# An attention and mixture-of-experts kernel: order of sums, row additions and one query projection in the attention part

## The reference

```python
xn = _layernorm(x, axis=-1)
# attention
q = einsum('bte,de->btd', xn, Wq) + bq;  k = ... + bk;  v = ... + bv
dot = einsum('bqd,bkd->bqk', q, k) / sqrt(256)
z = einsum('bqk,bkd->bqd', softmax(dot, axis=-1), v)
# experts
gates = softmax(xn @ Wg.T);  scores, inds = top_k(gates, 2);  scores = scores / sum(scores)
y = sum over the 2 chosen experts of score * (silu(g) * u) @ We_down
y = y + sigmoid(xn @ Wsg.T) * shared(xn)
out = x + z + y
```

## Time and profile before

| | us |
|---|---|
| median of 3 runs (lowest, highest) | 522.28 (521.79, 523.2) |
| the profiled execution | 520.53 |
| its span, first to last instruction | 518.4 |
| PE busy | 504.4 (97%) |
| DVE busy | 395.0 (76%) |
| ACT busy | 276.1 (53%) |
| POOL busy | 239.5 (46%) |

### The profile page before, as it was taken

The page is one execution under the profiler, slowest core; times in us unless marked ns, Lnnn a source line. Parts: engine busy times, 40 slices in busy tenths (PEclk is TensorE's granted clock), DMA queues, the critical chain, the costliest instruction groups (busy, mean ns, idle before and its releaser), DMA issues.

```text
span 518.4 us, 9986 instructions
## 1 busy us (share of the span) xinstructions
PE 504.4 (97%) x3347; PEld 458.1 (88%) x3347; DVE 395.0 (76%) x831; ACT 276.1 (53%) x473; POOL 239.5 (46%) x274
## 2 busy tenths in 40 slices
PE   8999999999999979999999999998999999999997
PEld 7898999988888969899998998897898989899887
DVE  5959454779999745766665744899897979797997
ACT  4767595524665424454444445565473727272742
POOL 0171585731100676756666503357735354554650
PEclk9999999999999988999999999999999999999999
DMA  8967668841112345549655746976225823722222
GB/s 298 408 222 265 235 212 310 326 134 57 36 56 62 113 133 164 173 147 312 194 166 167 139 121 205 357 195 228 81 87 174 298 57 87 219 87 61 73 62 71
DMA packets 48464, 88.05 MB, mean 170 GB/s; under 512 B 6080, under 2 KB 27200, under 8 KB 47392
## 3 DMA queue, kind: packets, MB, share of 16 engines
q1 hardware_dynamic: 40992, 68.58, 38.4%
q0 software_dynamic: 6864, 18.75, 14.0%
q10 hardware_dynamic: 560, 0.09, 0.1%
HBM read 51.72 MB, written 35.67 MB: 169 GB/s over the span
## 4 chain that ended last, share of the span: by engine, by line
PE 79%; DVE 14%; issue 5%; ACT 1%; POOL 0%; DVEq 0%; ACTq 0%
PE ps L867 45%; PE ps L1079 12%; PE ps L873 6%; PE ps L1009 6%; PE ps L1111 6%; DVE probs_f L1704 2%; DVE pT L1375 1%; PE ps L917 1%; PE ps L1026 1%; DVE top_keys L1679 1%; DVE acc L1719 1%; ACT scored_t L1174 1%; DVE sil L1446 1%; DVE place_hot L1560 1%; DVE less_wide L1696 1%
## 5 line engine op out<-in xcount | busy, mean ns | idle before, releaser
L854 POOL DMA_INDIRECT rows_y<-ytab,slot x64 | 80.9, 1264 | 71.8 <-DVE acc L1719 51.8
L824 POOL DMA_INDIRECT blk_x<-rows,row x79 | 82.2, 1040 | 64.0 <-DVE row L1575 22.7
L867 PEld LDWEIGHTS ps<-vv,pT 128*128 128x128 f32 x768 | 94.3, 189 | 5.0 <-DVE pT L1375 2.0
L867 PE MATMUL ps<-vv,pT 128*128 128x258 f32 x768 | 95.3, 283 | 3.4 <-DVE acc L1729 1.8
L867 PE MATMUL ps<-xT,shared_w 128*128 128x512 f32 x384 | 92.7, 394 | 0.8 <-DVE sil L1446 0.6
L867 PEld LDWEIGHTS ps<-xT,shared_w 128*128 128x128 f32 x384 | 70.5, 188 | 15.8 <-issue 1.6
L867 PE MATMUL ps<-qT,xbT_hi 128*128 128x512 f32 x256 | 79.1, 390 | 0.0
L1079 PE MATMUL ps<-expert_w,blk_xT 128*128 x474 | 67.9, 293 | 1.1 <-issue 0.4
L1079 PEld LDWEIGHTS ps<-expert_w,blk_xT 128*128 128x128 f32 x474 | 60.4, 193 | 5.1 <-issue 4.8
L1363 ACT ACTIVATE probs_f<-probs_f 128x1024 f32<-128x1024 f32 x32 | 33.8, 1058 | 47.0 <-DVE probs_f L1704 39.3
L867 PEld LDWEIGHTS ps<-qT,xbT_hi 128*128 128x128 f32 x256 | 47.1, 188 | 9.4 <-issue 0.2
(11 more groups left out here) (157 smaller groups left out, 827.1 us busy)
## 6 DMA issues: line engine op xcount, KB each, us to landing
ytab<-blk_y SPq DMA_DIRECT2D x40, 256.0 KB
keys<-xT SPq DMA_DIRECT2D x8, 1024.0 KB, 4.8
vals<-vals_out SPq DMA_DIRECT2D x32, 256.0 KB, 2.9
vv<-vals SPq DMA_DIRECT2D x8, 1024.0 KB, 10.8
stage_e<-in_experts SPq DMA_DIRECT2D x16, 384.0 KB
rows<-xn SPq DMA_DIRECT2D x8, 512.0 KB, 5.0
xbT_hi<-keys SPq DMA_DIRECT2D x8, 512.0 KB
xbT_lo<-keys SPq DMA_DIRECT2D x8, 512.0 KB
```

What stands on the lines that cost most here:

```text
L824: e.indirect_dma_start(out=blk_x[:, q, n, :], out_offset=None, in_=rows, in_offset=bass.IndirectOffsetOnAxis(ap=row[:, 2 * b + n:2 * b + n ...
L854: e.indirect_dma_start(out=rows_y[:, r, k, :], out_offset=None, in_=ytab, in_offset=bass.IndirectOffsetOnAxis(ap=slot[:, k, i:i + 1], axis=0),
L867: ins = e.matmul(dst, stationary(p, k), moving(q, k), start=(n == 0), stop=(n == total - 1))
```

## The change

It reorders steps and splits two kinds in two. `weigh_sum` (reciprocal and sum in one step) becomes `sum_invert` and `weigh_sum`; `rows_in` becomes `rows_first` and `rows_second`, so that another instruction can stand between the two of a pair. Then, in the groups:
1. In group 1 the row additions of tiles 2 and 3 no longer stand ahead of tile 1's sum.
2. In groups 1 to 6 the spread comes ahead of the sum of tile `old`+1, whose reciprocal follows the spread and whose sum follows the first `less`.
3. The projection of group 7's queries moves from group 5 to group 6.
4. Row additions, reciprocals, sums and low parts of different tiles alternate.

```diff
     def weigh(n):
-        return [("weigh", n), ("weigh_sum", n)]
+        return [("weigh", n), ("sum_invert", n), ("weigh_sum", n)]
+
+    def rows_around(i, *between):
+        return [("rows_first", i), *between, ("rows_second", i), *([("gather", i + YR)] if i + YR < TILES else [])]
 
     def rows(i):
-        return [("rows_in", i), *([("gather", i + YR)] if i + YR < TILES else [])]
+        return rows_around(i)
...
-    ahead = {g: split("heads", *divmod(g + 2, 2)) for g in range(1, GROUPS - 2)}
+    ahead = {g: split("heads", *divmod(g + 2, 2)) for g in range(1, GROUPS - 3)}
+    ahead[GROUPS - 2] = split("heads", *divmod(GROUPS - 1, 2))
...
-            steps += [("tops", g), *ahead.get(g, []),
-                      *([*rows(old + 2), *rows(old + 3)] if g == 1 else []), *weigh(old + 1), *spread(g), ("less", new), ("probs", new), ("less", new + 1),
-                      *spread_second(g), ("probs_hi", new), ("probs", new + 1), *rows(new),
-                      *weigh(old + 2), ("probs_hi", new + 1), ("less", new + 2), ("probs_lo", new), *rows(new + 1),
+            if g == 1:
+                tiles = (old + 2, old + 3, new + 1, new + 3)
+            else:
+                tiles = range(new, new + CT)
+            steps += [("tops", g), *ahead.get(g, []), ("weigh", old + 1), *spread(g), ("sum_invert", old + 1), ("less", new),
+                      ("weigh_sum", old + 1), ("probs", new), ("less", new + 1),
+                      *spread_second(g), ("probs_hi", new), ("probs", new + 1), ("weigh", old + 2),
+                      *rows_around(tiles[0], ("sum_invert", old + 2)), ("weigh_sum", old + 2),
+                      ("probs_hi", new + 1), ("less", new + 2), *rows_around(tiles[1], ("probs_lo", new)),
                       ("probs", new + 2), ("less", new + 3), ("probs_lo", new + 1)]
             if g + 2 < GROUPS:
-                steps += [("probs_hi", new + 2), *weigh(old + 3), ("probs", new + 3), ("probs_lo", new + 2), *rows(new + 2),
-                          ("probs_hi", new + 3), ("probs_lo", new + 3), *rows(new + 3)]
+                steps += [("probs_hi", new + 2), ("weigh", old + 3), ("probs", new + 3),
+                          *(rows(new) if g == 1 else []),
+                          *rows_around(tiles[2], ("sum_invert", old + 3)), ("weigh_sum", old + 3),
+                          ("probs_lo", new + 2), *(rows(new + 2) if g == 1 else []), ("probs_hi", new + 3),
+                          *rows_around(tiles[3], ("probs_lo", new + 3))]
             else:
-                steps += [*rows(new + 2), *rows(new + 3)]
+                steps += [*rows(tiles[2]), *rows(tiles[3])]
...
-                elif kind == "rows_in":
+                elif kind == "rows_first":
                     i, r = a[0], a[0] % YR
                     e.wait_ge(gathered[r], 16 * TOPK * (i // YR + 1))
                     e.wait_ge(biased, i + 1)
...
+                elif kind == "sum_invert":
                     n, w = a[0], a[0] % 2
                     e.wait_ge(weighed, n + 1)
                     if n >= 2:
                         e.wait_ge(z_added, n - 1)
                     e.reciprocal(rsum[:, w:w + 1], ps[:, sum_bank(n), D:D + 1]).then_inc(sum_inverted, 1)
+                elif kind == "weigh_sum":
+                    n, w = a[0], a[0] % 2
```

More of the change, by code:

```diff
@@ L272, in plan @@
         if last:
-            steps += [("probs_lo", new - 2), ("weigh", old - 1), *scores(g, 2), ("scores_max", g, 2), ("weigh_sum", old - 1)]
+            steps += [("probs_lo", new - 2), ("weigh", old - 1), *scores(g, 2), ("scores_max", g, 2), ("sum_invert", old - 1), ("weigh_sum", old - 1)]
         else:
@@ L301, in plan @@
             else:
-                steps += [*rows(new + 2), *rows(new + 3)]
+                steps += [*rows(tiles[2]), *rows(tiles[3])]
         else:
             steps += [("tops", g), ("probs", new - 1), ("probs_hi", new - 1), *weigh(old), ("probs_lo", new - 1),
-                      ("weigh", old + 1), *spread(g), ("less", new), ("less", new + 1), ("weigh_sum", old + 1),
+                      ("weigh", old + 1), *spread(g), ("less", new), ("less", new + 1), ("sum_invert", old + 1), ("weigh_sum", old + 1),
@@ L1715, in vector_program @@
                     e.wait_ge(biased, i + 1)
[L1716 to L1721, removed]
+                    e.scalar_tensor_tensor(out=acc[:, i, :], in0=rows_y[:, r, 0, :], scalar=score[:, 0, i:i + 1],
+                                           in1=acc[:, i, :], op0=ALU.mult, op1=ALU.add).then_inc(moe_added, 1)
+                elif kind == "rows_second":
+                    i, r = a[0], a[0] % YR
+                    e.wait_ge(moe_added, TOPK * i + 1)
+                    e.scalar_tensor_tensor(out=acc[:, i, :], in0=rows_y[:, r, 1, :], scalar=score[:, 1, i:i + 1],
+                                           in1=acc[:, i, :], op0=ALU.mult, op1=ALU.add).then_inc(moe_added, 1)
+                elif kind == "sum_invert":
                     n, w = a[0], a[0] % 2
```

## The result

| | before | changed |
|---|---|---|
| median, 9 runs each | 522.76 us (521.27 to 523.2) | 524.75 us (523.23 to 526.19) |
| ratio to before, 95% interval | 1 | 1.0043 (1.0027 to 1.0059) |
| profiled execution, its span | 520.53, 518.4 | 525.36, 523.3 |
| attention part in it, first scores to last matmul's end | 315.19 to 515.53 = 200.34 us | 316.67 to 520.35 = 203.68 us |

The forecast was 522.1 us and no change that can be measured. The medians differ by 2.0 us, more than the 1.6 us that the prediction took as the least to be told from no change (the interval reaches down to 1.4 us). The profiled executions differ by 4.83 us, more than the medians do. 1.48 us of it lies ahead of the attention part, in code that the change does not touch, where TensorE waits and its clock falls in both kernels (11 us from 185.00: TensorE busy 7.71 us before and 6.30 us changed).

A forecast was written before the change was run, and what follows sets the result against it. TensorE was taken as the bound in groups 2 to 6, so only its waits (3.86 us) counted. -0.47 - 1.93 + 2.12 + 0.1 = about -0.2 us from the 522.28 us median gave 522.1 us, range 519.8 to 524.0.

The forecast's parts named there:

- part 5: VectorE's dependent instructions set apart: some 0.6 us of its time a group, worth nothing; later gathers in group 1, no cost.
- the slower rival: Sum late in every group, through late gathers or a held spread; tiles 7, 11, 15 wait too: +2.3 us, 524.6 us; chance 0.12.
- Part 2: Groups 2 to 4, sum now behind a less: in group 2 0.66 us of slack left before tile 7, no cost.
- part 3: Group 5 without the queries' projection as cover: tile 19 waits for tile 17's sum, a new wait of 2.12 us.
- Part 1: Group 1, second sum ahead of the rows: tile 3 starts 0.47 us earlier.
- Part 4: The end: the wait before tile 28 goes, that before tile 30 falls to 0.13 us; 1.26 + 0.67 us won.
- The rival of no new wait in group 5: Tile 17's sum is there by 451.09, so the queries' move is pure gain: 2.4 us, 519.9 us; chance 0.20.
- every spread held: Each spread waits until both GpSimd reductions are over: +1.1 us, 523.4 us; chance 0.06.

The follow-up runs named there:

- heads_back: Changed kernel with the projection of group 7's queries put back into group 5: ratio to before 1.0021, attention part 201.88 us.
- sum_first: Changed kernel with the older sum ahead of the spread again in groups 1 to 6: ratio to before 0.9951, attention part 198.04 us.
- rows_early: Changed kernel with group 1's row additions of tiles 2 and 3 directly behind tile 1's sum: ratio to before 1.0029, attention part 202.71 us.
- best_a: Changed kernel with sums ahead of the spread and group 1's rows of tiles 2 to 6 earlier: ratio to before 0.9920, attention part 196.57 us.
- sum_mid: Changed kernel with tile 17's sum (group 5 alone) ahead of the first less: ratio to before 1.0012, attention part 201.10 us.
- changed_again: Changed kernel run once more, unaltered: ratio to before 1.0035, attention part 203.73 us.
- pairs_only: Changed kernel with sums, group 1's rows and queries placed as before, only the alternation left: ratio to before 0.9983, attention part 199.99 us.
- heads_only: Kernel before with only the projection of group 7's queries moved from group 5 to 6: ratio to before 0.9957, attention part 198.59 us.

## Why the prediction was wrong

**The step that failed is in part 5: "no cost" for the gathers**, argued with the rows of tiles 5 to 7 being read three or more large instructions after their gather's release. I had counted instructions where I should have counted time on GpSimd's queue, and for tile 7 the count was wrong too: between its gather's release and its first row addition VectorE has one large instruction (a low part of 1.21 us), not three. GpSimd after the change, columns as in the timelines above:

```profile
356.69 1.04 POOL L866 DMA_INDIRECT rows_y<-ytab,slot  x1 [4.14 <-DVE acc L1733]
...
360.33 2.89 POOL L866 DMA_INDIRECT rows_y<-ytab,slot  x1 [1.29 <-DVE acc L1733]
363.52 1.02 POOL L866 DMA_INDIRECT rows_y<-ytab,slot  x1 [0.30 <-issue]
364.85 1.73 POOL L866 DMA_INDIRECT rows_y<-ytab,slot  x1 [0.30 <-issue]
366.88 1.01 POOL L866 DMA_INDIRECT rows_y<-ytab,slot  x1 [0.30 <-issue]
```

The first gather of group 1, for tile 5, is issued at 356.69, against 351.75 before. The attention part began 1.48 us later, so that is 3.5 us later in it, under 4 us as forecast. But that for tile 7 is issued at 364.85 against 357.30, 6.1 us later in the same count, and not "under 4 us". Two instructions of 1.0 to 2.9 us belong to a gather, and they queue: that for tile 7 is released at 363.24 by tile 4's second row addition, issued from 364.85 and 366.88, and its rows can be read at 369.74, 6.5 us after the release: 1.6 us in the queue behind tile 6's gather, 3.0 us for the two issues, and 1.9 us more until the rows are there. (Why the issue at 360.33 takes 2.89 us is not shown.) VectorE in that time and up to tile 5's sum:

```profile
366.49 0.48 DVE L1728 SCALAR_TENSOR_TENSOR acc<-rows_y,score,acc 128x256 f32<-128x256 f32 x1 [0.80 <-DMA rows_y<-ytab,slot]
...
369.74 0.48 DVE L1728 SCALAR_TENSOR_TENSOR acc<-rows_y,score,acc 128x256 f32<-128x256 f32 x1 [2.25 <-DMA rows_y<-ytab,slot]
...
371.68 1.22 DVE L1688 TENSOR_TENSOR top_keys<-scored_t 128x1024 f32<-128x1024 f32 x1
...
376.78 0.69 DVE L1700 TENSOR_TENSOR top_keys<-top_keys,shift_wide 128x512 f32<-128x512 f32 x1
...
378.71 0.80 DVE L1708 TENSOR_TENSOR less_wide<-shift_wide,top_keys 128x256 f32<-128x256 f32 x1
...
380.69 0.48 DVE L1745 SCALAR_TENSOR_TENSOR acc<-ps,rsum,acc 128x256 f32<-128x256 f32 x1
```

It waits 0.80 + 2.25 = 3.05 us for rows. What could take this up ahead of group 2's maxima was VectorE's idle time there, and before the change that was 0.54 us:

```profile
371.18 1.22 DVE L1679 TENSOR_TENSOR top_keys<-top_keys,scored_t 128x1024 f32<-128x1024 f32 x1 [0.54 <-ACT scored_t L1174]
```

The prediction held 1.49 us of idle time against the slower rival, but read it in group 5. In group 2 3.05 - 0.54 = 2.5 us are left over, and so much is measured: the shifted maxima start 3.05 us after TensorE's tiles (376.78 against 373.73), where they had started 0.59 us after them, 2.46 us later in the group. Part 2 left a slack of 0.66 us, so 1.80 us of waiting is due, and 1.66 idle and 1.89 us in starts are measured. Part 2's order of time was right (the sum ends 3.70 us behind the maxima, 3.67 said) and its starting point was not. This is the slower rival's mechanism, in group 2 only: there it costs 1.89 us where I priced 0.24, or 0.7 for groups 2 to 4 together, while in groups 3 and 4 VectorE doesn't wait for rows. The experiments show it from several sides: it survives undoing the queries' move (heads_back) and three quarters of it survives the sum's old place (sum_first), but not the rows moved forward (rows_early), nor both together (best_a).

**A loss that stood in no part: the low clock behind tile 19.** The wait of part 3 was forecast at 2.12 us with its work behind it at full speed. It costs 2.09 + 1.58 us in the profile. In four profiles with a wait of 1.91 to 3.04 us there, 24 matmuls took 4.62 to 4.65 us; with 0.86 us (sum_mid) or none, they didn't. That it comes with the wait is shown by sum_mid, which moves one instruction, though on a chip of its own, and by mean clocks on one chip each: on that of changed_again (9 of 12 under 0.999) best_a without the wait had 1 of 8 and pairs_only 2 of 12; on that of rows_early (7 of 11) heads_back, heads_only and sum_first had none of 24. Whether the length of the wait decides it or also what runs around tile 19 is not shown, nor why it comes in some executions and not in others.

**What held.**
- Part 1: group 1's sum, with the wait before tile 3 at 1.35 (1.2 to 1.4 said) and 0.41 us won instead of 0.47. The spread took 0.80 us instead of the 0.67 assumed (group 0, where it starts later against the reductions; see the last section):

```profile
351.58 0.80 DVE L1708 TENSOR_TENSOR less_wide<-shift_wide,top_keys 128x256 f32<-128x256 f32 x1
352.30 0.15 DVE L1740 RECIPROCAL rsum<-ps 128x1 f32<-128x1 f32 x1
352.41 1.23 DVE L1716 TENSOR_TENSOR probs_f<-scored_t,less_wide 128x1024 f32<-128x1024 f32 x1
353.56 0.48 DVE L1745 SCALAR_TENSOR_TENSOR acc<-ps,rsum,acc 128x256 f32<-128x256 f32 x1
```

- Part 3: the wait itself, built from the row of group 6, came as in that row (1.20 and 0.84):

```profile
453.52 0.84 DVE L1708 TENSOR_TENSOR less_wide<-shift_wide,top_keys 128x256 f32<-128x256 f32 x1 [1.20 <-POOL top_keys L854]
454.39 1.23 DVE L1716 TENSOR_TENSOR probs_f<-scored_t,less_wide 128x1024 f32<-128x1024 f32 x1
455.53 0.48 DVE L1745 SCALAR_TENSOR_TENSOR acc<-ps,rsum,acc 128x256 f32<-128x256 f32 x1
```

- Part 4: both late waits are gone, and the first maximum of group 7 that needs a late copy now waits for it:

```profile
495.37 1.23 DVE L1691 TENSOR_TENSOR top_keys<-top_keys,scored_t 128x1024 f32<-128x1024 f32 x1 [0.78 <-ACT scored_t L1186]
```

  1.83 us is won at the end. That TensorE came later by more than thought did not undo it: the whole end shifted with it.
- Part 5 on the turns themselves: the pairs are worth 0.35 us in the profile of pairs_only, inside what can't be measured.
- The rival of no new wait in group 5 fell (1.91 us), and so did that of every spread held: in group 5 the spread ended at 454.36 while the reductions ran to 454.53.

**The mistake in the odds.** Both failures push the same way, and the range, 519.8 to 524.0, stopped short of the slower rival's 524.6. Its price was a sum over groups 2 to 5, which made it look like much to go wrong at once; one late gather, 3.05 us of waiting for rows, was enough, and a slack of 0.66 us is little against waits of that size. From 522.76, the median of before in the result, the -0.2 forecast and the 1.89 of tile 7 give 524.4 us, outside the range without any low clock; 0.5 us of that is only that this median is higher than the 522.28 the forecast started from.

## What to carry to other kernels

When a release is moved, follow what it releases to its landing, in time and not in instructions: queue of the issuing engine, its issues, the transfer. Here that was 6.4 to 6.9 us, and idle time of 0.54 us and slack of 0.66 us downstream had to pay. Idle time has to be read in the group that the delay falls into, not in another one like it. Two moves that each use the same cover must be priced together, since one can win alone and lose beside the other, as the move of the queries did here. A wait on TensorE that comes to about 2 us has to be priced with the durations behind it as well: look at the matmuls after it and at the granted clock, not at the idle time only.

## What the runs showed of the hardware

- A single wait of 1.91 us in TensorE's otherwise full stream was followed by about 3 us at the 1.2 GHz level; 24 matmuls took 4.65 us instead of 3.1. After waits of 0.71 to 1.77 us at other places of these kernels the next matmuls took 3.10 to 3.15 us for 24. By mean clock it came in at most nine of the twelve executions of changed_again, and perhaps in three of the nine of the result.
- A spread beside GpSimd's second reduction ends at a fixed time. In all eleven profiles, with the reductions taking 2.1 us, one that started 1.09 to 1.33 us after their start ended 1.93 to 1.97 us after it, so it took 0.84 down to 0.64 us; one that started 1.73 us after it took 0.42 us, the median of before (sum_first, best_a). That fits a spread that is held to about 1.5 us and then runs at its full speed as well as it fits one slowed throughout; no run tells them apart. What was wrong in the rival of the held spread is how long.
- A gather's two issues on GpSimd took 1.0 to 2.9 us each. Where VectorE waited for them, its rows were read 6.4 to 6.9 us after its buffer came free (changed kernel, sum_first, rows_early, best_a); 1.8 to 2.0 us of it passed behind the second issue, 3.9 us in rows_early.
